# Layer 1's expert stage in 160 tiles of two half tiles with separate experts, instead of 192 tiles of one expert each

## The chip, the cores and the metric

The kernel runs on one core of a Trainium2 chip. The metric is the device time of one execution in microseconds (us). Engines are named as in the profile: PE is TensorE (PEld its weight loads), DVE is VectorE, ACT is ScalarE, POOL is GpSimd, SP is SyncE, which here only issues transfers.

## The reference

Two layers, each a cross attention and a mixture of experts, on 2048 tokens of width 256. The change lies in the experts of layer 1:

```python
def _L1_ffn_ref(x, centroids, expert_biases, Ws_up, Ws_down, W_up, W_down):
    TOP_K = 8                                   # E = 64 experts, D = 256, F = 128, T = 2048
    xf = x.reshape(T, D)
    shared = jax.nn.silu(xf @ Ws_up) @ Ws_down
    aff = xf @ centroids.T
    _, idx = jax.lax.top_k(aff + expert_biases, TOP_K)
    w = jax.nn.sigmoid(jnp.take_along_axis(aff, idx, axis=1))
    w = w / (jnp.sum(w, axis=-1, keepdims=True) + 1e-08)
    cw = jnp.zeros((T, E)).at[jnp.arange(T)[:, None], idx].add(w)
    h = jax.nn.silu(jnp.einsum('td,edf->etf', xf, W_up))
    y = jnp.einsum('etf,efd->etd', h, W_down)
    return (shared + jnp.einsum('etd,te->td', y, cw)).reshape(B, S, D)
```

Each token goes to 8 of 64 experts, which makes 16384 rows of work. A row is a token of width 256, taken up to 128 by its expert, through silu, and back to 256.

## The kernel before, in words

Every engine runs its own instruction list, written out by hand; the lists meet in semaphores alone. During the attention of layer 1, POOL scatters every token's row, together with its 64 gates and 64 places (line 1805), into eight regions of `queue1`, one region per expert. Each region starts with padding rows, so that tiles of full size can be read from it. Then the expert stage runs over NX1 = 192 tiles of 128 rows. A short setup on PE and DVE works out which expert each tile belongs to (`expert_of`) and at which row of `queue1` it starts (`row_of`). The number of tiles is fixed; it doesn't depend on the data.

One tile passes through these steps:

1. SP reads 128 rows of `queue1` into the ring `g1` of 8 buffers (line 428).
2. PE transposes the tile in two halves of the width (`x1_T`, line 959), ACT copies it to `x1T` (line 1217).
3. DVE copies the expert's up weights into `w_now` (`weights_up`, line 1677), and also takes the place and the gate of each row from columns of `g1` that the expert's number picks (`places`, lines 1671 and 1672).
4. PE makes the up product, in which the weights are the stationary operand, so that the result h is already transposed (`up1`, line 974). ACT applies silu and writes `h1T` (line 1223).
5. PE makes the down product (`down1`, line 981), straight from `w_dn1`.
6. ACT (even tiles, line 1231) or DVE (odd tiles, line 1686) multiplies by the gate into the ring `y1` of 8 buffers.
7. POOL scatters the 128 rows to `routed1` by an indirect transfer (line 1848). Padding rows go to dump rows.

The order on PE in round j is up(j), transposes(j+2), down(j-2). The order on DVE is places(j), weights(j+1), and every second round an output. `w_now` holds two tiles' weights, and weights(j+1) waits for up(j-1) alone. Numbers of experts are loaded into registers of PE (line 963) and DVE (line 1689) 24 at a time, and rows' numbers into SP's registers 8 at a time (line 422). After the stage, SP reads the 8 rows of each token back and DVE adds them up (line 1714).

Of the kernel before, what the change touches and what calls it, by code (L numbers as in the profile page):

```python
# [26 lines left out]
P = 128  # L27
# [5 lines left out]
def build(nc, x, ctxT, mask, WqT, bq, Wk, bk, Wv, bv, w_routerT, gate_up, down, w_gateT, w_upT, w_downT,  # L33
# [20 lines left out]
    NX1 = 192  # L54
    assert NX0 >= E0 - 1 + TOK // P and NX1 >= E1 - 1 + TOK * TOP1 // P
# [8 lines left out]
    QROWS = P + TOK  # L64
    FAR = float(1 << 15)
    DUMPS = RING * P
    AHEAD = 16
    HELD = 24
    queue1 = nc.dram_tensor("queue1", [E1 * QROWS, XW], F32).ap()
    routed1 = nc.dram_tensor("routed1", [DUMPS + TOK * TOP1, D], F32).ap()  # L70

    ctx = ExitStack()
    with ctx:
# [8 lines left out]
        for shared, names in (  # L82
# [22 lines left out]
            ("gates1_steps", ("idx_y", "w_col")),  # L105
# [22 lines left out]
        for name, before in (("x1T_ps", "x0T_ps"), ("x1T", "x0T"), ("up1_ps", "eg0_ps"), ("w_now", "sg0x"), ("h1T", "e0T"),  # L128
                             ("dn1_ps", "dn0"), ("y1_1", "y0")):
            LATER[name] = (before, NX0)  # L130
# [32 lines left out]
        iota16 = sb("iota16", [P, NX1], F16)  # L163
        step128 = sb("step128", [P, NT])
        token_id = sb("token_id", [P, NT])
# [19 lines left out]
        ended = sb("ended", [P, NX1], F16)  # L185
# [7 lines left out]
        expert_of = sb("expert_of", [1, NX1], I32)  # L193
# [6 lines left out]
        pos1 = sb("pos1", [1, NX1])  # L200
# [3 lines left out]
        row_of = sb("row_of", [1, NX1], I32)  # L204
        w_col = sb("w_col", [P, AHEAD])
        idx_y = sb("idx_y", [P, AHEAD], I32)
        dump_at = sb("dump_at", [P, RING])
# [86 lines left out]
        g1, y1 = q(RING, XW), q(RING, D)  # L294
        x1T, w_now, h1T = q(2, KC, P), q(2, KC, F1), q(4, P)
        active1, began1, row_at = q(NX1), q(NX1), q(NX1)
# [38 lines left out]
        def _(sp):  # L335
# [22 lines left out]
            queue1_pads = queue1.rearrange("(e r) d -> r e d", e=E1)[0:P]  # L358
            sp.wait_ge(S("pads_made"), 1)
            for t in range(NT):  # L360
                sp.wait_ge(S("xs0"), nth("xs0", t + 1))
                sp.dma_start(scaled0[t * P:(t + 1) * P, :], xs0).then_inc(S("xs0_stored"), 16)
                at = slice(t * E1 // NT, (t + 1) * E1 // NT)
                sp.dma_start(queue1_pads[:, at], pads[:, :].unsqueeze(1).broadcast_to([P, E1 // NT, XW])).then_inc(S("pads_in"), 16)
# [55 lines left out]
            for j in range(NX1):  # L420
                if j % RING == 0:
                    _, at = nc.values_load_multi_w_load_instructions(row_of[0:1, j:j + RING], engines=(sp.engine,), min_val=0, max_val=E1 * QROWS - P,
                                                                     skip_runtime_bounds_check_because="the row names whole tiles of the regions alone")
# [9 lines left out]
            for t in range(NT):  # L433
                if t >= SUMS:
                    sp.wait_ge(S("final"), t - SUMS + 1)
                sp.dma_start(sums1[:, t % SUMS], routed1[DUMPS + t * P * TOP1:DUMPS + (t + 1) * P * TOP1, :].rearrange("(p k) d -> p k d", k=TOP1)).then_inc(S(f"sums_in{t % SUMS}"), 16)
# [93 lines left out]
        def _(pe):  # L530
# [417 lines left out]
            pe.matmul(bank(2)[:, 0:NX1], expert_rep[:, :], active1[0:E1, :], start=True, stop=True).then_inc(S("expert1_ps"), 1)  # L948
            pe.wait_ge(S("shift1"), nth("shift1", 1))
            pe.matmul(bank(0)[0:1, 0:NX1], tiles_of[0:E1, 3:4], active1[0:E1, :], start=True, stop=True).then_inc(S("row1_ps"), 1)  # L950
# [4 lines left out]
            def x1_T(j):  # L955
                k = j % RING
                pe.wait_ge(S(f"x1_in{k}"), nth(f"x1_in{k}", 16 * (j // RING + 1)))
# [4 lines left out]
            def experts(at):  # L962
                _, e = nc.values_load_multi_w_load_instructions(expert_of[0:1, at:at + HELD], engines=(pe.engine,), min_val=0, max_val=E1 - 1,
# [3 lines left out]
            def up1(j):  # L967
# [924 lines left out]
```

## Time and profile before

| | |
|---|---|
| median of 3 runs | 992.81 us (991.91 to 999.23) |
| profiled execution, its own time | 993.83 us |
| its span | 992.0 us |
| PE, DVE, ACT, POOL busy | 830.3, 558.5, 392.7, 408.9 us |
| expert stage of layer 1, first to last scatter of POOL | 692.57 to 936.89 us |
| sums after it | 937 to 992 us |

The chain that ended last spends 49% of the span on PE, 17% on DVE, 9% on POOL and 8% in transfers. Its shares are of the whole span, and the stages have different limits, so that the prediction reads the expert stage by itself.

### The profile page before, as it was taken

The numbers are of one execution on the slowest core, as the hardware profiler recorded it, in microseconds if no ns is written. First come the engines' busy times: TensorE is split into PE (matmuls) and PEld (weight loads), VectorE is DVE, ScalarE is ACT, GpSimd is POOL, SyncE is SP. The second block draws the span as 40 slices with busy tenths as digits, with TensorE's granted clock in tenths as the row PEclk, the third lists the DMA queues.
The fourth block names the chain that finished last, engine by engine and source line by source line (L and its number), as shares of the span: only waits on it lengthen the run. The fifth ranks groups of instructions, "written<-read, shape, count | busy, mean of one in ns | idle before, by whom it ended". The sixth has DMA issues, their size and how long they took to land.

```text
span 992.0 us, 21201 instructions
## 1 busy us (share of the span) xinstructions
PE 830.3 (84%) x6058; PEld 710.6 (72%) x6058; DVE 558.5 (56%) x1924; ACT 392.7 (40%) x1374; POOL 408.9 (41%) x467
## 2 busy tenths in 40 slices
PE   5899999789999998999999999854999998998300
PEld 4788887589999996677777777633988887787300
DVE  3666666512121123587878778641766666665288
ACT  1222222321111114655656665502766665565200
POOL 3100000031111002136676666562777777777600
PEclk9799999789999997899999999965999999999755
DMA  8123223489999972993233322238888887888397
GB/s 265 69 80 112 90 96 111 169 264 328 328 314 318 340 266 61 292 300 107 106 112 110 107 102 107 102 123 286 262 279 260 258 257 246 265 259 261 122 422 317
DMA packets 125103, 205.29 MB, mean 207 GB/s; under 512 B 13392, under 2 KB 100688, under 8 KB 122960
## 3 DMA queue, kind: packets, MB, share of 16 engines
q1 hardware_dynamic: 100880, 143.31, 44.8%
q0 software_dynamic: 19712, 56.65, 15.7%
q10 hardware_dynamic: 4416, 4.20, 1.3%
q8 instruction: 44, 0.72, 0.3%
q14 instruction: 51, 0.42, 0.1%
HBM read 132.93 MB, written 71.17 MB: 206 GB/s over the span
## 4 chain that ended last, share of the span: by engine, by line
PE 49%; DVE 17%; issue 11%; POOL 9%; DMA 8%; ACT 4%; DVEq 1%; SPq 1%; POOLq 0%; ACTq 0%
PE PS L739 10%; POOL routed L1848 7%; PE PS L749 5%; PE PS L974 4%; PE PS L981 4%; DVE R L1714 4%; PE PS L612 4%; DMA routed<-Q,idx_y 3%; PE PS L630 3%; PE PS L861 3%; PE PS L814 3%; ACT R L1152 2%; DMA R<-in_down 2%; PE PS L959 2%; DVE R L1488 2%
## 5 line engine op out<-in xcount | busy, mean ns | idle before, releaser
L1848 POOL DMA_INDIRECT routed<-Q,idx_y x192 | 187.1, 974 | 73.6 <-issue 46.3
L1805 POOL DMA_INDIRECT queue<-Q,slot x128 | 125.6, 981 | 78.2 <-DVE nmax L1482 49.7
L1152 ACT ACTIVATE R<-PS,nmax 128x154 f32<-128x154 f32 x256 | 108.4, 547 | 63.9 <-DVE nmax L1482 63.9
L974 PEld LDWEIGHTS PS<-Q 128*128 128x128 f32 x768 | 115.6, 193 | 25.1 <-ACT Q L1217 8.0
L974 PE MATMUL PS<-Q 128*128 128x128 f32 x768 | 119.5, 279 | 9.8 <-issue 5.5
L981 PE MATMUL PS<-R,Q 128*128 x384 | 118.3, 390 | 8.1 <-ACT Q L1223 5.1
L739 PEld LDWEIGHTS PS<-R 128*128 128x128 f32 x992 | 118.0, 196 | 6.0 <-issue 4.6
L739 PE MATMUL PS<-R 128*128 128x128 f32 x992 | 119.0, 279 | 2.9 <-DMA R<-in_down 1.8
L1677 DVE COPY Q<-R 128x256 f32 x192 | 60.5, 315 | 49.6 <-PE PS L974 29.8
L959 PE MATMUL PS<-ident,Q 128*128 128x128 f32 x384 | 74.5, 277 | 14.6 <-DMA Q<-queue 14.6
L1760 POOL TENSOR_TENSOR rstd<-var_eps,neg_half 128x1 f32<-128x1 f32 x32 | 17.7, 554 | 159.9 <-DVE var_eps L1312 159.7
L1217 ACT ACTIVATE Q<-PS 128x256 f32<-128x256 f32 x192 | 74.0, 385 | 23.9 <-PE PS L959 23.5
L1442 DVE TENSOR_TENSOR R<-R,PS 128x512 f32<-128x512 f32 x31 | 21.4, 689 | 109.4 <-PE PS L739 109.4
L1686 DVE TENSOR_SCALAR Q<-PS,w_col 128x256 f32<-128x256 f32 x96 | 46.3, 482 | 56.1 <-DMA routed<-Q,idx_y 40.2
L1785 POOL DMA_INDIRECT R<-scaled,idx x32 | 30.6, 955 | 106.4 <-PE PS L725 97.9
L1223 ACT ACTIVATE Q<-PS 128x128 f32<-128x128 f32 x192 | 53.0, 276 | 44.6 <-PE PS L974 42.0
L981 PEld LDWEIGHTS PS<-R,Q 128*128 128x128 f32 x384 | 58.1, 191 | 14.7 <-issue 13.9
L612 PE MATMUL PS<-R 128*128 128x128 f32 x512 | 65.4, 282 | 0.0
L1231 ACT ACTIVATE Q<-PS,w_col 128x256 f32<-128x256 f32 x96 | 45.5, 474 | 45.2 <-DMA routed<-Q,idx_y 35.0
L612 PEld LDWEIGHTS PS<-R 128*128 128x128 f32 x512 | 61.5, 196 | 0.1
L959 PEld LDWEIGHTS PS<-ident,Q 128*128 128x128 f32 x384 | 49.0, 144 | 15.5 <-DMA Q<-queue 15.5
L1152 ACT ACTIVATION_READ_ACCUMULATOR R<-PS,nmax 128x1 f32 x256 | 59.3, 232 | 0.0
(269 smaller groups left out, 1568.2 us busy)
## 6 DMA issues: line engine op xcount, KB each, us to landing
Q<-queue SPq DMA_DIRECT2D x192, 192.0 KB
R<-in_gate_up SPq DMA_DIRECT2D x31, 1024.0 KB, 6.6
R<-routed SPq DMA_DIRECT2D x16, 1024.0 KB, 18.2
R<-in_down SPq DMA_DIRECT2D x31, 512.0 KB, 8.8
queue<-pads SPq DMA_DIRECT2D x16, 768.0 KB, 3.6
R<-in_W_up SPq DMA_DIRECT2D x16, 512.0 KB, 7.3
R<-in_W_down SPq DMA_DIRECT2D x8, 1024.0 KB, 11.2
routed<-R SPq DMA_DIRECT2D x31, 128.0 KB
```

The lines of the kernel that those rows point to most:

```text
L612: i = pe.matmul(bank(b)[:, f * P:(f + 1) * P], w[:, c, f * P:(f + 1) * P], xn2T[:, c, :], start=(c == 0), stop=(c == KC - 1))
L739: i = pe.matmul(bank(2 * half + p)[:, f * P:(f + 1) * P], expert_w[k % WB][0][:, c, at:at + P], x0T[:, p, c, :], start=(c == 0), stop=(c = ...
L749: i = pe.matmul(bank(6 + p)[:, 0:D], e0T[:, p, f, :], expert_w[k % WB][1][:, f, :], start=(f == 0), stop=(f == FC0 - 1))
L959: i = pe.transpose(bank(j % 2)[:, c * P:(c + 1) * P], g1[:, k, c * P:(c + 1) * P], ident[:, :])
L974: i = pe.matmul(bank(2 + p)[:, 0:P], w_now[:, p, c, :], x1T[:, p, c, :], start=(c == 0), stop=(c == KC - 1))
L981: pe.matmul(bank(6 + j % 2)[:, 0:D], h1T[:, j % 4, :], w_dn1[:, bass.ts(e, 1), :], start=True, stop=True).then_inc(S("dn1_ps"), 1)
L1152: i = act.activation(prob[:, g % 2].rearrange("p (k h) -> p h k", h=HG)[:, h, :], src, ACT.Exp, bias=nmax2[:, g % 2, h:h + 1], accum_out=d ...
L1217: act.activation(x1T[:, j % 2].rearrange("p c n -> p (c n)"), bank(j % 2)[:, 0:D], ACT.Copy).then_inc(S("x1T"), 1)
L1223: act.activation(h1T[:, j % 4, :], bank(2 + j % 2)[:, 0:P], ACT.Silu).then_inc(S("h1T"), 1)
L1677: dve.tensor_copy(w_now[:, j % 2].rearrange("p c f -> p (c f)"), w_up1[:, bass.ts(e, 1)].rearrange("p o c f -> p (o c f)")).then_inc(S("w_ ...
L1805: pool.indirect_dma_start(out=queue1, out_offset=bass.IndirectOffsetOnAxis(ap=slot1[:, t * TOP1 + k:t * TOP1 + k + 1], axis=0), in_=pay[:, ...
L1848: pool.indirect_dma_start(out=routed1, out_offset=bass.IndirectOffsetOnAxis(ap=idx_y[:, a:a + 1], axis=0), in_=y1[:, k], in_offset=None).t ...
```

## The change: what it does

A tile now is two halves of 64 rows, and each half can belong to any expert. An expert's rows are rounded up to 64 instead of 128, so that 320 half tiles, 160 tiles, hold all of them. What follows from that in the code:

- SP reads each half with a transfer of its own.
- The up product has the tokens as stationary operand: for each half and each half of the width one matmul with 64 stationary columns, four per tile. Its output has tokens in its rows. The first half's weights are read straight from `w_up1`, the second half's from `w_now`.
- ACT's silu writes `h1`; PE transposes it (`h1_T`, line 986), and DVE copies the transpose to `h1T` (line 1701).
- The down product is two matmuls with 64 stationary columns, again with the first half's weights in place and the second half's in `w_now`.
- `w_now` now holds up and down weights of the second half's expert, 512 numbers per partition, for 5 tiles (`weights_b`, line 1695).
- Gate and place lie side by side and are copied by one DVE instruction per half. Padding rows carry a place out of bounds, and POOL's scatter drops them.
- All outputs are ACT's.
- Registers with experts' numbers are loaded 16 at a time, for 8 tiles, by PE and by DVE; SP loads 16 row numbers for 8 tiles.

The order of the instruction lists changes as follows. `ISA` is the sequencer's work on an address that a register holds. The names in the waits are those of reused semaphores: x0T stands for `x1T`, sg0x for `w_now`, e0T for `h1T`, y0 for the outputs, rows_out and rows_in for the loads and scatters of a ring buffer, gates1_steps for places and gates, eg0_ps for the up product, dn0 for the down product, and in the new kernel eu0_ps for `h1`.

PE, one round of the expert stage, before:

```order
L974 MATMUL PS<-Q 128x128 [waits e0T,sg0x,x0T]
L974 MATMUL PS<-Q 128x128
L959 MATMUL PS<-ident,Q 128x128 [waits rows_out1]
L959 MATMUL PS<-ident,Q 128x128
L981 ISA [waits y0,e0T]
L981 MATMUL PS<-R,Q 128x256
```

PE, one round, now:

```order
L976 ISA [waits sg0x,eu0_ps,x0T]
L976 MATMUL PS<-R,Q 64x128
L978 MATMUL PS<-Q 64x128
L976 ISA
L976 MATMUL PS<-R,Q 64x128
L978 MATMUL PS<-Q 64x128
L961 MATMUL PS<-ident,Q 128x128 [waits rows_out7]
L961 MATMUL PS<-ident,Q 128x128
L986 MATMUL PS<-ident,Q 128x128 [waits e0T,eu0_ps]
L992 ISA [waits y0,e0T]
L992 MATMUL PS<-R,Q 64x256
```

Between the transposes of x and the down product there is now the transpose of h of two tiles earlier, and the down product is that of three tiles earlier. Line 993, the second half's down product, follows.

DVE, the same place of the program, before:

```order
L1671 ISA [waits rows_out3]
L1671 TENSOR_SCALAR idx_y<-Q,dump_at 128x1
L1672 ISA
L1672 COPY w_col<-Q 128x1
L1677 ISA [waits eg0_ps]
L1677 COPY Q<-R 128x256
```

DVE, one round with the load of registers in it, now:

```order
L1701 COPY Q<-PS 128x128 [waits dn0,h1T_ps]
L1689 ISA [waits rows_in7,rows_out7]
L1689 COPY gate_place<-Q 64x2
L1689 ISA
L1689 COPY gate_place<-Q 64x2
L1704 TENSOR_LOAD expert_of
L1695 ISA [waits dn0]
L1695 COPY Q<-R 128x512
```

The copy of h (line 1701, of tile j-2) now stands ahead of the gates of tile j and of the weights of tile j+1 (line 1695). It waits for PE's transpose in the same round. The load stands between gates and weights.

The core of the diff:

```diff
-    NX1 = 192
+    H = P // 2
+    NX1 = 160
+    NH1 = 2 * NX1
...
-    HELD = 24
+    HELD = 8
+    LAG = 3
+    WNOW = LAG + 2
...
                 if j >= RING:
                     sp.wait_ge(S("x1T_ps"), nth("x1T_ps", j - RING + 1))
-                    sp.wait_ge(S("w_col"), nth("w_col", j - RING + 1))
-                sp.dma_start(g1[:, k, :], queue1[bass.ds(at[k], P), :]).then_inc(S(f"x1_in{k}"), 16)
+                    sp.wait_ge(S("w_col"), 2 * (j - RING + 1))
+                for a in range(2):
+                    sp.dma_start(g1[a * H:(a + 1) * H, k, :], queue1[bass.ds(at[2 * k + a], H), :]).then_inc(S(f"x1_in{k}"), 16)
...
-            def up1(j):
+            def up1(j, e):
                 p = j % 2
                 pe.wait_ge(S("x1T"), nth("x1T", j + 1))
+                if j >= 2:
+                    pe.wait_ge(S("h1"), nth("h1", j - 1))
                 pe.wait_ge(S("w_now"), nth("w_now", j + 1))
+                for c in range(KC):
+                    pe.matmul(bank(2 + p)[0:H, 0:F1], x1T[:, p, c, 0:H], w_up1[:, bass.ts(e[2 * j], 1), c, :].rearrange("p o f -> p (o f)"),
+                              start=(c == 0), stop=(c == KC - 1), skip_group_check=True)
+                    i = pe.matmul(bank(2 + p)[H:P, 0:F1], x1T[:, p, c, H:P], w_now[:, j % WNOW, 0, c * F1:(c + 1) * F1],
+                                  start=(c == 0), stop=(c == KC - 1), skip_group_check=True)
+                i.then_inc(S("up1_ps"), 1)
+
+            def h1_T(j):
+                pe.wait_ge(S("h1"), nth("h1", j + 1))
                 if j >= 2:
                     pe.wait_ge(S("h1T"), nth("h1T", j - 1))
-                for c in range(KC):
-                    i = pe.matmul(bank(2 + p)[:, 0:P], w_now[:, p, c, :], x1T[:, p, c, :], start=(c == 0), stop=(c == KC - 1))
-                i.then_inc(S("up1_ps"), 1)
+                pe.transpose(bank(4 + j % 2)[:, 0:P], h1[:, j % 4, :], ident[:, :]).then_inc(S("h1T_ps"), 1)
...
-            for j in range(NX1 + 2):
+            for j in range(NX1 + LAG):
+                if j < NX1:
+                    up1(j, e)
                 if j % HELD == HELD - 1 and j + 1 < NX1:
                     e += experts(j + 1)
-                if j < NX1:
-                    up1(j)
                 if j + 2 < NX1:
                     x1_T(j + 2)
-                if j >= 2:
-                    down1(j - 2, e[j - 2])
+                if 2 <= j < NX1 + 2:
+                    h1_T(j - 2)
+                if j >= LAG:
+                    down1(j - LAG, e)
...
-            def weights_up(j, e):
-                if j >= 2:
-                    dve.wait_ge(S("up1_ps"), nth("up1_ps", j - 1))
-                dve.tensor_copy(w_now[:, j % 2].rearrange("p c f -> p (c f)"),
-                                w_up1[:, bass.ts(e, 1)].rearrange("p o c f -> p (o c f)")).then_inc(S("w_now"), 1)
...
+            def weights_b(j, e):
+                if j >= WNOW:
+                    dve.wait_ge(S("dn1_ps"), nth("dn1_ps", j - WNOW + 1))
+                pair = R[:, 0:NUP + E1 * D].rearrange("p (m e f) -> p e m f", m=2, e=E1)
+                dve.tensor_copy(w_now[:, j % WNOW], pair[:, bass.ts(e, 1)].rearrange("p o m f -> p (o m) f")).then_inc(S("w_now"), 1)
+
+            def h1_T(j):
+                dve.wait_ge(S("h1T_ps"), nth("h1T_ps", j + 1))
+                if j >= 4:
+                    dve.wait_ge(S("dn1_ps"), nth("dn1_ps", j - 3))
+                dve.tensor_copy(h1T[:, j % 4, :], bank(4 + j % 2)[:, 0:P]).then_inc(S("h1T"), 1)
...
-            for j in range(NX1 + 3):
+            for i in range(PAY):
+                dve.wait_ge(S(f"queued{i}"), 16 * TOP1 * (NT // PAY))
+            weights_b(0, e[1])
+            for j in range(NX1 + 2):
+                if j >= 2:
+                    h1_T(j - 2)
                 if j < NX1:
-                    places(j, e[j % HELD])
+                    places(j, e[2 * (j % HELD):2 * (j % HELD) + 2])
                     if j % HELD == HELD - 1 and j + 1 < NX1:
                         e = experts(j + 1)
                 if j + 1 < NX1:
-                    weights_up(j + 1, e[(j + 1) % HELD])
-                if j >= 3 and j % 2 == 0:
-                    out_x1(j - 3)
+                    weights_b(j + 1, e[2 * ((j + 1) % HELD) + 1])
...
-                pool.indirect_dma_start(out=routed1, out_offset=bass.IndirectOffsetOnAxis(ap=idx_y[:, a:a + 1], axis=0),
-                                        in_=y1[:, k], in_offset=None).then_inc(S(f"placed{k}"), 16)
+                pool.indirect_dma_start(out=routed1, out_offset=bass.IndirectOffsetOnAxis(ap=gate_place[:, a, 1:2].bitcast(I32), axis=0),
+                                        in_=y1[:, k], in_offset=None, bounds_check=FIRST + TOK * TOP1 - 1, oob_is_err=False).then_inc(S(f"placed{k}"), 16)
```

## Rows read from the trace of the kernel before

**Rows 1.** Busy time by stage; columns as in the first line, x counts instructions.

```profile
core 0: us, PE busy (x) PEld busy (x) DVE busy (x) ACT busy (x) POOL busy (x), PEclk, DMA share, GB/s
693.00:937.00 244.00, 217.19 (x1503) 195.53 (x1502) 148.41 (x722) 147.02 (x469) 185.78 (x192) 0.99 0.78 249
937.00:992.00 55.00, 0.00 (x0) 0.00 (x0) 43.87 (x64) 0.00 (x0) 0.86 (x1) 0.50 0.86 348
```

**Rows 2.** The scatter's line: durations in ns, then idle time before it (us, times).

```profile
L1848 POOL DMA_INDIRECT routed<-Q,idx_y x192: 963/969/1090, 692.6 to 936.9; - x192
  issue: 46.3, 152
```

**Rows 3.** Timeline of POOL: start us, us, engine, line.

```profile
692.57 0.96 POOL L1848 DMA_INDIRECT routed<-Q,idx_y  x1 [15.34 <-ACT Q L1231]
...
935.62 0.96 POOL L1848 DMA_INDIRECT routed<-Q,idx_y  x1 [0.30 <-issue]
936.89 0.97 POOL L1848 DMA_INDIRECT routed<-Q,idx_y  x1 [0.30 <-issue]
```

**Rows 4.** Timeline of PE in the expert stage, one round.

```profile
711.36 0.61 PE L974 MATMUL PS<-Q 128*128 128x128 f32 x4
711.80 0.38 PE L959 MATMUL PS<-ident,Q 128*128 128x128 f32 x2
712.02 0.60 PE L981 MATMUL PS<-R,Q 128*128 x2
712.46 0.61 PE L974 MATMUL PS<-Q 128*128 128x128 f32 x4
```

**Rows 5.** Timeline of the attention of layer 1, around matmuls with 32 stationary columns.

```profile
620.92 0.39 PE L844 MATMUL PS<-R,Q 104*128 104x128 f32 x2
621.24 0.43 PE L846 MATMUL PS<-R,Q 128*32 128x128 f32 x8
621.59 0.66 PE L855 MATMUL PS<-ident,R 128*128 128x128 f32 x4
622.29 0.69 DVE L1501 TENSOR_TENSOR R<-R,PS 128x512 f32<-128x512 f32 x1 [0.54 <-PE PS L855]
```

**Rows 6.** Timeline of DVE in the expert stage, weights, places, weights.

```profile
715.17 0.29 DVE L1677 COPY Q<-R 128x256 f32 x1 [1.84 <-issue]
715.38 0.21 DVE L1671 TENSOR_SCALAR idx_y<-Q,dump_at 128x1 int32 x1
715.51 0.15 DVE L1672 COPY w_col<-Q 128x1 f32 x1
715.65 0.29 DVE L1677 COPY Q<-R 128x256 f32 x1
```

**Rows 7.** The line of the weights' copy: durations in ns, shape.

```profile
L1677 DVE COPY Q<-R x192: 277/294/545, 684.8 to 923.6; 128x256 f32 x192
```

**Rows 8.** Timeline around a load of registers, PE's weight loads and DVE.

```profile
742.69 0.52 PEld L974 LDWEIGHTS PS<-Q 128*128 128x128 f32 x4 [1.71 <-issue]
...
745.08 0.29 DVE L1677 COPY Q<-R 128x256 f32 x1 [1.92 <-issue]
...
745.44 0.52 PEld L974 LDWEIGHTS PS<-Q 128*128 128x128 f32 x4 [1.78 <-issue]
```

**Rows 9.** Timeline, PE's gap at another load of registers.

```profile
714.47 0.52 PEld L974 LDWEIGHTS PS<-Q 128*128 128x128 f32 x4 [1.16 <-ACT Q L1217]
```

**Rows 10.** Register loads by line: durations in ns (min/median/max).

```profile
L963 PEldq TENSOR_LOAD <-expert_of x8: 1771/1830/2156, 682.7 to 894.9; - x8
L1689 DVEq TENSOR_LOAD <-expert_of x8: 1720/1946/2333, 682.8 to 895.1; - x8
L422 SPq TENSOR_LOAD <-row_of x24: 521/564/871, 682.4 to 906.4; - x24
```

**Rows 11.** Busy time in the attention of layer 1 and after it.

```profile
620.00:640.00 20.00, 18.21 (x158) 13.84 (x159) 14.54 (x39) 11.11 (x50) 10.94 (x12) 1.00 0.28 102
740.00:747.00 7.00, 4.25 (x29) 3.38 (x29) 2.65 (x14) 3.15 (x11) 5.48 (x6) 1.00 0.69 221
651.00:660.00 9.00, 5.22 (x14) 3.16 (x12) 2.69 (x9) 0.19 (x1) 3.98 (x5) 0.50 0.20 76
```

**Rows 12.** ACT's and PE's groups in the expert stage, busy us, mean ns.

```profile
L1217 ACT ACTIVATE Q<-PS 128x256 f32<-128x256 f32 x187 | 72.0, 385 | 0.0
...
L1223 ACT ACTIVATE Q<-PS 128x128 f32<-128x128 f32 x189 | 52.1, 276 | 43.9 <-PE PS L974 41.3 <-issue 2.1
...
L1231 ACT ACTIVATE Q<-PS,w_col 128x256 f32<-128x256 f32 x96 | 45.5, 474 | 45.2 <-DMA routed<-Q,idx_y 35.0 <-DVE w_col L1672 4.5 <-DVE idx_y L1671 2.0
```

More of the change, by code:

```diff
@@ L53, in build @@
     COLS0 = 32
[L54 to L55 removed]
+    H = P // 2
+    NX1 = 160
+    NH1 = 2 * NX1
+    assert NX0 >= E0 - 1 + TOK // P and NH1 >= E1 - 1 + TOK * TOP1 // H
     RING = 8
@@ L127, in build @@
             LATER[f"placed{k}"] = (f"rows_in{k}", 16 * GROUPS0)
-        for name, before in (("x1T_ps", "x0T_ps"), ("x1T", "x0T"), ("up1_ps", "eg0_ps"), ("w_now", "sg0x"), ("h1T", "e0T"),
-                             ("dn1_ps", "dn0"), ("y1_1", "y0")):
+        for name, before in (("x1T_ps", "x0T_ps"), ("x1T", "x0T"), ("up1_ps", "eg0_ps"), ("w_now", "sg0x"), ("h1", "eu0_ps"), ("h1T", "e0T"),
+                             ("dn1_ps", "dn0"), ("y1", "y0")):
             LATER[name] = (before, NX0)
@@ L421, in _ @@
                 if j % RING == 0:
-                    _, at = nc.values_load_multi_w_load_instructions(row_of[0:1, j:j + RING], engines=(sp.engine,), min_val=0, max_val=E1 * QROWS - P,
-                                                                     skip_runtime_bounds_check_because="the row names whole tiles of the regions alone")
+                    _, at = nc.values_load_multi_w_load_instructions(row_of[0:1, 2 * j:2 * (j + RING)], engines=(sp.engine,), min_val=0, max_val=E1 * QROWS - H,
+                                                                     skip_runtime_bounds_check_because="the row names whole half tiles of the regions alone")
                 k = j % RING
@@ L979, in down1 @@
                 if j >= 2:
-                    pe.wait_ge(S(f"y1_{j % 2}"), nth(f"y1_{j % 2}", j // 2))
-                pe.matmul(bank(6 + j % 2)[:, 0:D], h1T[:, j % 4, :], w_dn1[:, bass.ts(e, 1), :], start=True, stop=True).then_inc(S("dn1_ps"), 1)
+                    pe.wait_ge(S("y1"), nth("y1", j - 1))
+                pe.matmul(bank(6 + j % 2)[0:H, 0:D], h1T[:, j % 4, 0:H], w_dn1[:, bass.ts(e[2 * j], 1), :], start=True, stop=True, skip_group_check=True)
+                i = pe.matmul(bank(6 + j % 2)[H:P, 0:D], h1T[:, j % 4, H:P], w_now[:, j % WNOW, 1, :], start=True, stop=True, skip_group_check=True)
+                i.then_inc(S("dn1_ps"), 1)
             pe.wait_ge(S("w1_in"), 16 * (E1 // 8) * (KC + 1))
@@ L1239, in _ @@
                     x1_T(j + 2)
-                if j >= 2 and j % 2 == 0:
-                    out_x1(j - 2)
+                if j >= LAG:
+                    out_x1(j - LAG)
             for t in range(NT):
@@ L1628, in _ @@
             step("count1")
-            dve.tensor_scalar(small[0:E1, 0:NT], step128[0:E1, :], count, 0.0, ALU.is_lt, ALU.add, accum_out=ntiles).then_inc(S("ntiles1"), 1)
+            dve.tensor_scalar(small[0:E1, 0:2 * NT], step64[0:E1, :], count, 0.0, ALU.is_lt, ALU.add, accum_out=ntiles).then_inc(S("ntiles1"), 1)
             step("ntiles1")
@@ L1672, in places @@
[L1672 to L1686 removed]
+                for h in range(2):
+                    own = slice(h * H, (h + 1) * H)
+                    both = g1[own, k, D:XW].rearrange("p (two e) -> p e two", two=2)[:, bass.ds(e[h], 1), :]
+                    dve.tensor_copy(gate_place[own, a, :], both.rearrange("p o two -> p (o two)")).then_inc(S("w_col"), 1)
```

94 lines of the change are left out of this document (41 added, 53 removed).

## The prediction

> **What bounds the kernel now.** I read the busy time by stage first, to cut the expert stage out of the span. It is 244 us long, and no engine fills it: PE's records cover 217 us, POOL's 186 [rows 1]. Then the scatter's own line, since POOL waits there least: one scatter takes 0.97 us, and in 152 of 192 cases 0.30 us follow in which POOL waited for nothing the profile shows [rows 2]. The timeline makes that a beat: the last two scatters start at 935.62 and 936.89, 1.27 us apart. From the first, at 692.57, to the last there are 191 intervals in 244.3 us, 1.28 each [rows 3]. So POOL's scatter sets the pace of the whole stage. PE could go a little faster: its round takes 712.46 - 711.36 = 1.10 us [rows 4]. After the stage come 55 us of sums [rows 1], which the change leaves as they are.
>
> If nothing else came to bind, 160 scatters at 1.28 instead of 192 would save 32 x 1.28 = 41 us. The question is whether the new round can be kept within 1.28 us.
>
> **The new round has a closed loop.** The lists show it without any timing. PE's up product of tile j+1 waits for the weights of tile j+1. DVE makes these last in its round j, behind the copy of h of tile j-2, and that copy waits for PE's transpose of h in round j. That transpose stands behind up(j) and the transposes of x. So PE's first part (up, two transposes of x, transpose of h) and DVE's part (copy of h, two gate copies, weights) alternate; they never overlap. The five buffers of `w_now` don't help, as the order on DVE, not the buffers, holds the weights back. Before, weights(j+1) waited only for up(j-1), and no such loop was there. One turn of the loop, step by step:
>
> - Weights written to first weight load on PE: DVE's copy that starts at 745.08 and takes 0.29 ends at 745.37, PE loads at 745.44 [rows 8]. 0.07 us.
> - The up product. Nothing before has 64 stationary columns. The nearest row is the attention's block of eight records with 32 columns: it starts at 621.24, and the next block with the full array starts at 621.59, 0.35 later, where eight records in line at the 0.11 of rows 4 (four of L974 in 711.80 - 711.36 = 0.44) would need 0.88 [rows 4, 5]. So tiles of the array side by side run together, four at a time: two beats of 0.11, and the rest (0.13) is filling and the change between a split and a full array. With 64 columns two run together, so the up product's eight records take four beats: 0.35 + 2 x 0.11 = 0.57 us to the next full block. I add 0.05 for the first weight loads that nothing hides. From below: no such extra and no cost of changing the split, 0.44. From above: halves that don't overlap, 0.88 + 0.13 = 1.01; this is a rival below.
> - Three transposes and the way to DVE. Four transposes started at 621.59, and DVE's reader started at 622.29, 0.70 later [rows 5]. Three make 0.70 - 0.11 = 0.59.
> - DVE from the copy of h to the start of the weights' copy: from 715.17 to 715.65 there is the same pattern, one copy, two small operations with an address in a register, one copy: 0.48 us [rows 6]. The first copy was 256 wide from SBUF, here it is 128 wide from PSUM; the four instructions' issue sets this time (0.13 between the small ones), so I take it as it is.
> - The weights' copy, now 512 wide. 256 take 0.294 [rows 7], 1 takes 0.15 [rows 6]: the slope gives 0.294 + 0.145 = 0.44. Upper end 0.59, twice the row.
>
> Sum: 0.07 + 0.05 + 0.57 + 0.59 + 0.48 + 0.44 = 2.20 us per tile. Bounds of the sum: 2.0 (the low up product, the rest of DVE 0.05 faster) and 2.4 (the copy at 0.59 and a little more latency).
>
> **Beside the loop, at no cost.** Two down matmuls (0.44 plus a change of the array's split) run while DVE has the turn, 0.92 us. ACT has 0.385 + 0.276 + 0.474 = 1.14 us per tile [rows 12], POOL 1.28, SP two transfers instead of one; all are below 2.20, and their feeds are three tiles apart. POOL's waits vanish from the path, and so do the waits for landed scatters. DVE's sums of gates, every tenth tile, fall into its idle half of the loop. If the loop were cut, POOL would be next at 1.28, and PE at about 1.4 (0.44 + 0.22 + 0.11 + 0.44 and two changes of the split). The padding, the wider setup rows (320 instead of 192) and POOL's extra constant cost below 1 us.
>
> **Loads of registers.** Before, 24 numbers took 1.83 us on PE and 1.95 on DVE, 8 numbers 0.56 on SP [rows 10]. Sixteen should take about 1.2. They now come every 8 tiles, 19 times, and both stand in the loop: PE's between up and the transposes, DVE's between gates and weights. They follow each other, as at 742.69 and 745.44, where PE stood 1.71 and then 1.78 us [rows 8]. Of a load of 24, DVE lost 1.92 [rows 8], nearly all, and PE 1.16 where its queue was full [rows 9]. For 16 I take 1.1 on DVE and 0.9 on PE: 2.0 x 19 = 38 us. Bounds 1.3 and 3.0 per pair: 25 to 57 us. In the kernel before, the slack against POOL's beat paid for most of this.
>
> **Sum.** First scatter: three rounds later in the order instead of two and longer rounds, +2.5 us. Then 159 x 2.20 = 350 and 38. Together 390.5 against 244.3: +146. The profiled execution took 993.83 us, so 1140; it lies 1 us above the median of the runs shown, and I keep **1140 us**. With the bounds: 2.5 + 318 + 25 - 244 = +101, 1095 us; 2.5 + 382 + 57 - 244 = +197, 1191 us.
>
> **Rivals.**
> 1. *POOL still sets the beat* (faster). If DVE's list ran ahead of PE's transposes, the round would be 1.28 and the time 993.8 - 41 + 3 = 955 us. For it speaks that each engine alone has less work than 2.2 us; against it, that the order is fixed in both lists. The new kernel ties with the old at a turn of (244.3 - 2.5 - 38) / 159 = 1.28 us with the loads, and of 241.8 / 159 = 1.52 us if the loads cost nothing; below that it is faster. No bound of the loop comes near either. Chance 4%, and 2% that it ends within 1%.
> 2. *The halves don't overlap on PE.* Each up product takes 0.44 longer, +70 us: 1210 us. Against it are rows 5, though these have 32 columns. 6%.
> 3. *TensorE's clock falls to 1.2 GHz.* In a turn of 2.20 us PE streams 0.44 + 0.33 + 0.44 = 1.21 us, 55%, and in a round with loads 1.21 of 4.2. The granted clock was 1.00 in a stretch where PE's records covered 18.2 of 20 us, and also in 7 us with 4.25 us covered, around two stalls; it was 0.50 only where 14 matmul records stand in 9 us [rows 11]. At half the clock, the 0.77 us of streaming in the loop would double: 0.77 x 159 = +122, 1262 us for the whole stage, about 1180 if a third of it is hit. 13%, most of it for a part of the stage.
> The Trainium skill, "TensorE: Matmul & The Clock Gate", Part 4 on the PE-mode transpose, says that transposes don't count as busy the way matmuls do. By that rule the stage would look emptier than it is, since three of its beats are transposes, and rival 3 would be the forecast. The attention of layer 1, with its many transposes, kept 1.00 [rows 11], so I leave it a rival.
> 4. *The loop is shorter than its parts*, because I count latencies twice: a turn of 1.5 to 1.9 us, 1030 to 1090 us. 7%.
>
> **Numbers.** Forecast (1095 to 1191) 68%, rivals as above. The range takes in rival 2 and the milder part of rival 3: **1085 to 1215**. A change of this kernel is told from none at about 1%. Faster by over 1%: 0.04; within 1%: 0.02; slower by over 1%: 0.94.
>
> **What would show it.** Scatters 2.2 us apart with POOL waiting for ACT, ACT for PE; PE's idle time in front of the up product (line 976) put down to DVE's copy of weights (line 1695), and DVE's idle time in front of line 1701 put down to PE's transpose (line 986); both about 0.9 us or more per tile. The eight records of the up product within about 0.6 us would confirm the overlap; 1 us would be rival 2. Gaps of about 1 us on both engines every 8 tiles for the loads. Clock 1.00 in the stage. The prediction is wrong if DVE's weights are done before PE's transpose of the same round.

## The result and the profile after

| | before | changed |
|---|---|---|
| median, both on one chip | 993.76 us (4 runs, 991.91 to 999.23) | 1274.47 us (4 runs, 1265.88 to 1278.06) |
| profiled execution, its own time | 993.83 us | 1277.72 us |
| first to last scatter of the expert stage | 244.3 us | 521.7 us |

The ratio is 1.281, with a 95% interval of 1.278 to 1.285. The change made the kernel slower, as forecast, but by 281 us and not by 146; the time lies 59 us above the range.

The first view is again the busy time by stage, of the changed kernel. It answers to [rows 1].

```profile
core 0: us, PE busy (x) PEld busy (x) DVE busy (x) ACT busy (x) POOL busy (x), PEclk, DMA share, GB/s
0.00:684.00 684.00, 607.32 (x4522) 508.77 (x4522) 363.79 (x1122) 240.77 (x893) 221.84 (x275) 0.94 0.53 171
684.00:1219.00 535.00, 450.46 (x2400) 229.88 (x2400) 172.06 (x706) 182.30 (x481) 154.45 (x158) 0.56 0.30 91
1219.00:1276.00 57.00, 0.00 (x0) 0.00 (x0) 43.87 (x64) 0.23 (x1) 2.28 (x3) 0.51 0.82 331
```

The stage carries the whole difference: the sums after it still take about 55 us. Two things stand in its row. DVE, ACT and POOL are busy for less than 35% each, so none of them has too much work. And the granted clock is 0.56 on average, where it was 0.99. Cut finer, the same view shows that it has two values and nothing between:

```profile
892.90:1118.20 225.30, 196.19 (x979) 99.54 (x981) 69.25 (x285) 73.93 (x196) 63.68 (x65) 0.50 0.29 91
1118.20:1135.20 17.00, 11.81 (x105) 6.24 (x101) 7.50 (x31) 7.51 (x21) 6.84 (x7) 1.00 0.42 128
```

TensorE ran at 1.2 GHz (0.50) for 225 us in a row, then 17 us at 2.4 GHz (1.00). In the 17 us it issued 105 matmuls, 6.2 per us; in the long stretch 4.3 per us, the same work per turn in longer turns.

Next the groups of the expert stage by line: busy us and mean ns of one, then the idle time ahead of them and what ended it.

```profile
L976 PE MATMUL PS<-R,Q 128*64 x640 | 166.9, 411 | 74.1 <-DVE Q L1695 74.1
...
L1866 POOL DMA_INDIRECT routed<-Q,gate_place x160 | 156.7, 980 | 388.2 <-ACT Q L1246 373.6 <-issue 14.6
...
L1701 DVE COPY Q<-PS 128x128 f32<-128x128 f32 x160 | 46.5, 291 | 325.8 <-PE PS L986 325.8
```

PE waits for DVE's weights in front of the up product, DVE waits for PE's transpose of h in front of its copy, and POOL, which set the pace before [rows 2, 3], stands idle for 388 us. The closed loop is there as the prediction drew it. DVE waits 325.8 / 160 = 2.04 us per tile. PE's own wait reads as only 74.1 / 160 = 0.46 us, half of the 0.9 that was forecast for both engines, because at 1.2 GHz its records are longer and cover most of the time in which DVE has the turn: ahead of the up product that starts at 806.39, at full clock, it is 0.72 us, and ahead of the one at 907.46, at half clock, 0.25.

Here is one turn at full clock, from the timeline: the first weight load of the up product, the transposes of x, DVE's copy of h, its two gate copies, the weights' copy, and the next turn's first weight load.

```profile
806.39 0.13 PEld L976 LDWEIGHTS PS<-R,Q 128*64 128x64 f32 x1 [1.17 <-issue]
...
806.99 0.20 PEld L961 LDWEIGHTS PS<-ident,Q 128*128 128x128 f32 x2 [0.17 <-issue]
807.57 0.29 DVE L1701 COPY Q<-PS 128x128 f32<-128x128 f32 x1 [1.42 <-PE PS L986]
807.78 0.36 DVE L1689 COPY gate_place<-Q 64x2 f32 x2
...
808.17 0.43 DVE L1695 COPY Q<-R 128x512 f32 x1
808.84 0.13 PEld L976 LDWEIGHTS PS<-R,Q 128*64 128x64 f32 x1 [1.18 <-issue]
```

And one at half clock:

```profile
904.21 0.18 PEld L976 LDWEIGHTS PS<-R,Q 128*64 128x64 f32 x1 [1.07 <-issue]
...
905.26 0.29 PEld L961 LDWEIGHTS PS<-ident,Q 128*128 128x128 f32 x2 [0.33 <-issue]
906.20 0.29 DVE L1701 COPY Q<-PS 128x128 f32<-128x128 f32 x1 [2.24 <-PE PS L986]
906.41 0.35 DVE L1689 COPY gate_place<-Q 64x2 f32 x2
906.79 0.43 DVE L1695 COPY Q<-R 128x512 f32 x1
907.46 0.18 PEld L976 LDWEIGHTS PS<-R,Q 128*64 128x64 f32 x1 [1.07 <-issue]
```

Read against the prediction's terms, with the median over all turns of that kind without a load of registers (16 at full clock, 117 at half clock) in the last two columns:

| step of the turn | forecast | 806.39 | 904.21 | median, full | median, half |
|---|---|---|---|---|---|
| weights written to first weight load | 0.07 + 0.05 | 0.24 | 0.24 | 0.24 | 0.24 |
| up product, to the transposes | 0.57 | 0.60 | 1.05 | 0.60 | 1.06 |
| transposes, to DVE's copy of h | 0.59 | 0.58 | 0.94 | 0.58 | 0.94 |
| copy of h, to the weights' copy | 0.48 | 0.60 | 0.59 | 0.59 | 0.59 |
| the weights' copy | 0.44 | 0.43 | 0.43 | 0.43 | 0.43 |
| turn | 2.20 | 2.45 | 3.25 | 2.44 | 3.25 |

DVE's steps are the same at both clocks; PE's two steps grow from 1.18 to 2.00. The turns with a load of registers take 4.17 us at full clock (4 of them) and 4.61 at half (15), which is 1.73 and 1.36 us more.

### The profile page after: what moved, and what is told of

Its sections match the earlier page's. It is cut to its first block, busy times and chain, and to the rows that moved or that the text cites. A ratio compares the mean times of both kernels' runs of the same rounds, so it can differ in the third digit from the quotient of the medians.

```text
span 1275.9 us, 23745 instructions
## 1 busy us (share of the span) xinstructions
PE 1057.8 (83%) x6922; PEld 738.6 (58%) x6922; DVE 579.7 (45%) x1892; ACT 423.3 (33%) x1374; POOL 378.6 (30%) x435
## 4 chain that ended last, share of the span: by engine, by line
PE 55%; DVE 20%; issue 13%; ACT 3%; DMA 3%; DVEq 3%; POOL 1%; SPq 1%; POOLq 0%; ACTq 0%
PE PS L976 12%; PE PS L741 8%; PE PS L961 7%; DVE Q L1695 5%; PE PS L751 4%; DVE R L1731 3%; PE PS L614 3%; PE PS L986 3%; PE PS L632 2%; PE PS L816 2%; PE PS L863 2%; DVE gate_place L1689 2%; ACT R L1167 2%; DVE R L1503 1%; PE PS L592 1%
## 5 line engine op out<-in xcount | busy, mean ns | idle before, releaser
L1866 POOL DMA_INDIRECT routed<-Q,gate_place x160 | 156.7, 980 | 388.2 <-ACT Q L1246 373.6
L976 PE MATMUL PS<-R,Q 128*64 x640 | 166.9, 411 | 74.1 <-DVE Q L1695 74.1
L976 PEld LDWEIGHTS PS<-R,Q 128*64 128x64 f32 x640 | 107.2, 205 | 194.7 <-issue 194.5
L1701 DVE COPY Q<-PS 128x128 f32<-128x128 f32 x160 | 46.5, 291 | 325.8 <-PE PS L986 325.8
L978 PE MATMUL PS<-Q 128*64 128x128 f32 x640 | 167.8, 413 | 0.0
L992 PE MATMUL PS<-R,Q 128*64 x320 | 165.6, 618 | 0.8 <-DVE Q L1701 0.8
L993 PE MATMUL PS<-Q 128*64 128x256 f32 x320 | 165.5, 618 | 0.0
L741 PEld LDWEIGHTS PS<-R 128*128 128x128 f32 x992 | 117.9, 195 | 5.0 <-issue 2.3
L1246 ACT ACTIVATE Q<-PS,gate_place 128x256 f32<-128x256 f32 x160 | 75.7, 473 | 128.7 <-PE PS L993 126.5
L978 PEld LDWEIGHTS PS<-Q 128*64 128x64 f32 x640 | 107.3, 206 | 0.0
L1695 DVE COPY Q<-R 128x512 f32 x160 | 68.3, 427 | 37.4 <-PE PS L993 17.1
L992 PEld LDWEIGHTS PS<-R,Q 128*64 128x64 f32 x320 | 43.9, 195 | 49.2 <-issue 48.8
```

The source lines that it names most:

```text
L741: i = pe.matmul(bank(2 * half + p)[:, f * P:(f + 1) * P], expert_w[k % WB][0][:, c, at:at + P], x0T[:, p, c, :], start=(c == 0), stop=(c = ...
L976: pe.matmul(bank(2 + p)[0:H, 0:F1], x1T[:, p, c, 0:H], w_up1[:, bass.ts(e[2 * j], 1), c, :].rearrange("p o f -> p (o f)"), start=(c == 0), ...
L978: i = pe.matmul(bank(2 + p)[H:P, 0:F1], x1T[:, p, c, H:P], w_now[:, j % WNOW, 0, c * F1:(c + 1) * F1], start=(c == 0), stop=(c == KC - 1), ...
L992: pe.matmul(bank(6 + j % 2)[0:H, 0:D], h1T[:, j % 4, 0:H], w_dn1[:, bass.ts(e[2 * j], 1), :], start=True, stop=True, skip_group_check=True)
L993: i = pe.matmul(bank(6 + j % 2)[H:P, 0:D], h1T[:, j % 4, H:P], w_now[:, j % WNOW, 1, :], start=True, stop=True, skip_group_check=True)
L1246: act.activation(y1[:, k], bank(6 + j % 2)[:, 0:D], ACT.Copy, scale=gate_place[:, j % AHEAD, 0:1]).then_inc(S("y1"), 1)
```

## The experiments

Every kernel was timed beside the kernel before on the same chip, and the ratios are to that. Each short diff is against the changed kernel unless it says otherwise.

### The loop cut: weights of the next tile first

```diff
-                    places(j, e[2 * (j % HELD):2 * (j % HELD) + 2])
-                    if j % HELD == HELD - 1 and j + 1 < NX1:
-                        e = experts(j + 1)
-                if j + 1 < NX1:
-                    weights_b(j + 1, e[2 * ((j + 1) % HELD) + 1])
+                    places(j, old[2 * (j % HELD):2 * (j % HELD) + 2])
```

with the load and `weights_b(j + 1, ...)` moved ahead of `h1_T(j - 2)` on DVE. Nothing else is changed.

> The changed kernel with one reordering on DVE: in round j the weights of tile j+1 are copied first, then h of tile j-2, then the gates. Nothing is left out. Theory (a loop of PE and DVE makes PE idle, and the idle PE is granted 1.2 GHz): DVE's trip gets two PE rounds, so the next bound is PE's own work with 64-column halves, about 1.5 us per tile by the full-clock rounds of the changed kernel (0.60 up, 0.48 to the down product, 0.49 down). Clock 1.00 in the stage, 159 x 1.5 + 15 for loads = 254 us between first and last scatter, 1005 us in all (980 to 1030). Rival (matmuls on 64 columns themselves don't hold the clock, however dense): clock about 0.5 in the stage, a PE round near 2.6 us, 1180 us or more.

Measured: 1010.87 us, ratio 1.019 (1.016 to 1.022). The scatters run from 694.10 to 953.24, and the stage's row is

```profile
694.00:953.00 259.00, 240.60 (x2339) 154.97 (x2335) 170.80 (x690) 172.34 (x468) 159.96 (x159) 1.00 0.60 182
```

with the groups

```profile
L1867 POOL DMA_INDIRECT routed<-Q,gate_place x160 | 160.9, 1006 | 119.2 <-issue 64.6 <-ACT Q L1246 54.6
...
L976 PE MATMUL PS<-R,Q 128*64 x640 | 99.3, 278 | 7.4 <-DVE Q L1695 7.1
```

One change of order on DVE was worth 264 of the 281 us. PE's wait for weights falls from 74.1 to 7.4 us, the clock is 1.00 throughout, and PE is now covered for 240.6 of 259 us. On DVE, two turns look so:

```profile
746.44 0.43 DVE L1695 COPY Q<-R 128x512 f32 x1
...
747.24 0.29 DVE L1701 COPY Q<-PS 128x128 f32<-128x128 f32 x1 [0.37 <-PE PS L986]
747.44 0.35 DVE L1689 COPY gate_place<-Q 64x2 f32 x2
...
747.94 0.43 DVE L1695 COPY Q<-R 128x512 f32 x1
```

The weights' copies start 1.50 us apart, PE's own round now. But this run doesn't say how much was the loop at full clock and how much was the clock, since both went together. The next one holds the loop and changes only the clock.

### The loop kept, TensorE given work in its idle time

```diff
+                if j < NX1:
+                    if j:
+                        pe.wait_ge(S("h1"), nth("h1", j))
+                    for _ in range(2):
+                        pe.matmul(bank(2 + (j + 1) % 2)[:, 2 * P:3 * P], ident[:, :], ident[:, :], start=True, stop=True, skip_group_check=True)
```

at the end of PE's round: two 128x128 products that nobody reads, in the time in which DVE has the turn.

> The changed kernel, order untouched, plus two 128x128 matmuls on the full array per round behind the down product, whose result nobody reads. Theory (low use of PE, made by the loop, costs the clock): the filler runs while DVE has its turn, the clock stays at 1.00, and the round is the 2.44 us that the changed kernel shows at full clock: 159 x 2.44 + 19 x 1.7 = 420 us between the scatters, 1170 us in all (1150 to 1195), 100 us faster than without the filler although PE does more. Rival (the clock has another cause): no gain, 1275 to 1300 us.

Measured: 1183.57 us, ratio 1.192 (1.188 to 1.197). With more work for PE the kernel is 91 us faster than the change. Its stage:

```profile
695.00:1127.00 432.00, 381.64 (x2970) 232.56 (x2966) 169.09 (x691) 177.54 (x469) 156.78 (x159) 0.97 0.36 109
```

The granted clock is 0.97 instead of 0.56, and 128 turns at full clock have a median of 2.45 us, those of the change at full clock. So the 281 us divide into 190 for the loop at (nearly) full clock and 91 for the clock.

### The same with transposes as the filler

```diff
+                    for _ in range(4):
+                        pe.transpose(bank(2 + (j + 1) % 2)[:, 2 * P:3 * P], ident[:, :], ident[:, :])
```

in the place of the two products.

> The changed kernel with filler again, as in the filler kernel and at its place, but four transposes of 128x128 instead of two matmuls; both stream for 0.44 us at full clock. If the clock follows PE's use whatever is streamed: clock about 1.00 in the stage and 1184 us like the matmul filler. If transposes don't count as use, as the Trainium skill says on the PE-mode transpose: the clock stays as low as without filler, PE's added work gets longer, and the time is 1275 us or more.

Measured: 1182.17 us, ratio 1.191 (1.187 to 1.195), and

```profile
695.00:1127.00 432.00, 372.81 (x2968) 216.66 (x2966) 169.65 (x691) 177.52 (x469) 157.08 (x159) 0.97 0.36 109
```

Transposes held the clock as the products did, 0.97. The Trainium skill ("TensorE: Matmul & The Clock Gate", Part 4, on the PE-mode transpose) says of the bf16 transposes measured there that they don't count as busy in the same way. By that rule this kernel, with fp32 transposes, would have kept the change's clock of 0.56; it did not, and the measurement decides. Rival 3 came true, but not for the reason for which the prediction quoted that page. What the change lacked was work on PE between its turns, and either kind would do.

### Half a cut: places and gates behind the weights

```diff
-                if j < NX1:
-                    places(j, e[2 * (j % HELD):2 * (j % HELD) + 2])
...
+                if j < NX1:
+                    places(j, old[2 * (j % HELD):2 * (j % HELD) + 2])
```

The gates move behind `weights_b(j + 1, ...)`; the copy of h stays ahead of it, so the loop stays closed.

> The changed kernel with the two gate copies moved behind the weights on DVE; copy of h still ahead of the weights, so the loop stays, 0.35 us shorter (0.59 to about 0.24 between the copy of h and the weights). Loop theory: 159 x 0.35 = 55 us less at the clock as it is, 1220 us; if the denser PE is granted the full clock for longer, down to 1110. Rival (DVE's order doesn't matter, since PE's matmuls set the round): no change, 1275 us.

Measured: 1162.71 us, ratio 1.171 (1.167 to 1.176), between the two expected values. The turn without a load is 2.21 us at full clock (median of 94) and 2.99 at half; the step from the copy of h to the weights is 0.32 instead of 0.59. The stage's clock:

```profile
697.00:1107.00 410.00, 304.03 (x2346) 161.72 (x2342) 176.74 (x691) 177.53 (x469) 156.25 (x160) 0.90 0.38 115
```

The gates cost 0.27 us of the turn, of which some is lost again to weights' copies that now take longer (next section). 159 x 0.27 = 43 us would be the most at an unchanged clock, but the kernel gained 112 against the change, with full clock in most of the stage (0.90 on average instead of 0.56). A few tenths in a loop moved the clock, and the clock moved more time than they did.

### The loop put into the kernel before

```diff
+                if 1 <= j < NX1 - 1:
+                    dve.wait_ge(S("x1T_ps"), nth("x1T_ps", j + 2))
```

in `weights_up` of the kernel before (diff against that): DVE's weights of tile j+1 now also wait for PE's transposes of tile j+2, which stand behind up(j) in PE's list. It does no work of the change.

> The kernel before with one wait more on DVE: the weights of tile j+1 wait for PE's transposes of tile j+2 in round j, so that the same kind of loop exists without half tiles. Loop theory: a turn of 0.07 + 0.93 on PE + 0.1 + 0.29 on DVE = 1.4 us against POOL's 1.28, 192 x 1.4 + 20 for loads, which are in the loop now, = 290 us for 244: 1040 us (1020 to 1060), clock 1.00, as PE still streams 1.1 of 1.4 us. Rival (POOL or PE hides it): 994 us.

Measured: 1071.73 us, ratio 1.080 (1.075 to 1.084). The wait alone costs 79 us, and the expectation was too low by 12 us at its upper end. In the timeline of DVE the turns differ:

```profile
731.19 0.29 DVE L1679 COPY Q<-R 128x256 f32 x1 [1.66 <-PE PS L959]
...
732.70 0.29 DVE L1679 COPY Q<-R 128x256 f32 x1 [1.01 <-PE PS L959]
732.91 0.48 DVE L1688 TENSOR_SCALAR Q<-PS,w_col 128x256 f32<-128x256 f32 x1
733.30 0.20 DVE L1671 TENSOR_SCALAR idx_y<-Q,dump_at 128x1 int32 x1
733.42 0.14 DVE L1672 COPY w_col<-Q 128x1 f32 x1
734.21 0.51 DVE L1679 COPY Q<-R 128x256 f32 x1 [0.64 <-PE PS L959]
```

The weights come 1.51 us apart here, and PE's up products start at 731.59, 733.09 and 734.82, 1.50 and then 1.73 apart: a turn with an output (L1688) in it is followed by a weights' copy of 0.51 instead of 0.29 and a later product. The expectation had 1.4 us for every turn; without an output it is 1.51, and the turns with one were not priced at all. The longer copy falls into a scatter of POOL, here the one that starts 0.55 us before it:

```profile
733.66 0.97 POOL L1850 DMA_INDIRECT routed<-Q,idx_y  x1 [1.80 <-DVE Q L1688]
```

In this kernel 80 of the 192 weights' copies start 0.5 to 0.6 us after a scatter did; they take 0.51 us (median), and none of the other 112 takes more than 0.30. In the kernel with the gates moved, 70 of 160 copies start 0.5 to 0.8 us after a scatter did, and every one of them ends 1.23 us after the scatter's start, whenever it began, so that they take 0.43 to 0.70 us. A copy that starts in the second half of a scatter is thus held until 0.1 to 0.25 us after the scatter's recorded end. In the change only one weights' copy starts within a scatter, and all take 0.43. The clock stayed at 0.99 in this kernel, so it is a measure of a loop alone.

### What bounds it once the loop is cut: the loads

The cut kernel's turn is 1.50 us, and 2.2 in every eighth. Here PE loads the first halves' experts only, 8 numbers from a row of their own, on top of the cut:

```diff
-                _, e = nc.values_load_multi_w_load_instructions(expert_of[0:1, 2 * at:2 * (at + HELD)], engines=(pe.engine,), min_val=0, max_val=E1 - 1,
+                _, e = nc.values_load_multi_w_load_instructions(expert_a[0:1, at:at + HELD], engines=(pe.engine,), min_val=0, max_val=E1 - 1,
```

> The kernel with the weights first on DVE, and PE loads only what it needs, the expert of each first half: 8 numbers instead of 16 per 8 tiles, from a row of its own. Nothing is left out. If loads of registers stand in PE's path, where that kernel's round with a load took 2.34 us against 1.50: a load of 0.56 instead of 1.11 us gives back 19 x 0.5 = 10 us: 1001 us (997 to 1006). Rival (the round with a load is long because of DVE's own load of 16): no change, 1011 us.

Measured: 1013.01 us, ratio 1.020 (1.017 to 1.023): no change against the cut kernel's 1.019. PE's load did become 0.61 us, and the turn with the load is still 2.17 us. DVE's load, still of 16 numbers, accounts for most of it: PE waits 9.5 us for DVE's weights in the stage (23 waits), and 19 turns that are 0.67 us too long make 13 us. The two loads:

```profile
L966 PEldq TENSOR_LOAD <-expert_a x20: 590/612/1018, 681.5 to 937.6; - x20
...
L1706 DVEq TENSOR_LOAD <-expert_of x20: 1095/1241/1457, 681.5 to 937.3; - x20
```

### Two tiles per round

```diff
-    LAG = 3
-    WNOW = LAG + 2
+    LAG = 4
+    WNOW = 7
...
+            for j in range(0, NX1 + LAG, 2):
+                for i in (j, j + 1):
+                    if i < NX1:
+                        up1(i, e)
```

and so on for every step of PE, ACT and DVE, with the weights first and PE's short load: the array would change its split half as often.

> The same kernel with two tiles per round on PE, ACT and DVE: two up products, then four transposes of x, two of h, then two down products; w_now has 7 buffers, the lag is 4 tiles. Nothing is left out. If PE's own work, with the changes between the split and the full array, is what bounds the weights-first kernel (1.50 us per tile): one pair of changes per two tiles instead of per tile saves 0.1 us, 159 x 1.40 + 19 x 0.5 + 4 = 236 us between the scatters, 985 us (970 to 998), under both kernels. Rival (the two waits inside a round on DVE or ACT bind instead): 1000 us or more.

Measured: 1033.31 us, ratio 1.041 (1.039 to 1.044), slower than the cut kernel by 22 us where 26 less were expected. On DVE, with two weights' copies in a row:

```profile
802.29 0.49 DVE L1712 COPY Q<-PS 128x128 f32<-128x128 f32 x2 [0.42 <-PE PS L989]
802.69 0.88 DVE L1700 COPY gate_place<-Q 64x2 f32 x4
803.61 0.76 DVE L1706 COPY Q<-R 128x512 f32 x2
805.67 0.49 DVE L1712 COPY Q<-PS 128x128 f32<-128x128 f32 x2 [1.30 <-issue]
```

The pair takes 3.38 us, 1.69 per tile, where the cut kernel takes 1.50. PE's up product waits 41.9 us in the stage: 22.5 for DVE's weights and 19.1 for ACT. So the coarser hand-over between the engines cost more than fewer changes of the split can have bought; what those bought by themselves no run shows.

### Weights two tiles ahead

On top of the kernel with PE's short load:

```diff
-    WNOW = LAG + 2
+    WNOW = LAG + 3
...
+            weights_b(1, e[3])
...
+                if j + 2 < NX1:
+                    weights_b(j + 2, e[2 * (j + 2) + 1])
```

> The weights-first kernel with PE's short load, and DVE's weights copied two tiles ahead instead of one (6 buffers of w_now); DVE's load of 16 numbers so comes one round earlier too. Nothing is left out. With one tile ahead, PE's rounds are 1.50 us, but 2.2 us every eighth, where DVE loads registers for 1.2 us. If it is DVE's load that PE meets there: the second tile of lead covers it, 19 x 0.6 = 11 us less, 1002 us, and 995 if the rounds of 1.65 us in between shorten too. Rival (these rounds are long for another reason, PE's own queue or the outputs): no change, 1013 us.

Measured: 1079.39 us beside 1072.33 for the kernel before, ratio 1.006 (1.004 to 1.009). The chip was another one, on which the kernel before itself took 79 us longer than on the others. So this ratio can't be set against the 1.020 of above, and both kernels went once more, together:

> The kernel of x8 (weights copied two tiles ahead, TensorE loads 8 numbers), now on the same chip as x5's kernel. If the second weights' place ahead of the loop is what one tile more of distance buys, the loads' long turns (2.17 us against 1.5) shrink to 1.5 and seven or eight us of the loop go: ratio to the kernel before 1.00 to 1.01 where x5 had 1.0199, and about 0.013 below x5's kernel of this call. If another wait has taken the turn over (ScalarE's output copies, or the scatters), both have the same ratio within 0.004.

> The kernel of x5 again, as the measure of x9 on this chip: ratio to the kernel before 1.017 to 1.023 as it was, if the chip is like the first; on a chip whose transfers are slower, nearer to 1.00, since the stages ahead then weigh more and the scatters hide the loop.

Measured, on yet another chip, where the kernel before takes 1084.41 us: two ahead 1085.54 us, ratio 1.001 (0.998 to 1.003); one ahead 1090.41 us, ratio 1.005 (1.002 to 1.007). The ratios are 0.0039 apart where the first theory expected 0.013, and their intervals touch. On this chip that is the second theory's answer, though only just within its 0.004. But here the whole stage is longer, for a reason that stays open (below), and that can hide what the second tile of distance buys. The kernel with weights two tiles ahead was never timed on a chip like the first, so whether it gives back the 11 us there stays open. On such a slow chip the cut kernel with PE's short load is within 1% of the kernel before. No version of the change beat it anywhere.

### The two kernels once more

> The kernel before, unchanged, for its profile on whatever chip this call gets: on two chips it took 1072 and 1084 us instead of 993. If the chip is such a one, its expert stage should be 50 to 60 us longer at the same busy time of each engine, as it is in x9 and x10; if it is one like the first, the span is 992 us again.

> The change unchanged. On a chip like the first, 1274 us and ratio 1.28. On one where the kernel before takes 1075 us: if what such a chip adds falls into the changed loop's idle times, about 1300 us and a ratio of 1.21; if it adds to the loop, 1350 us and 1.26.

Measured, on another chip, where the kernel before is as fast as at first: it took 992.35 us (one run), the change 1291.12 us (4 runs) beside 992.32 (7 runs), ratio 1.300 (1.294 to 1.306). What the slow chips add could not be seen. But the change took 17 us more than the first time, and the row of its stage says why:

```profile
684.00:1235.00 551.00, 480.58 (x2400) 243.03 (x2400) 170.73 (x705) 182.43 (x481) 154.30 (x158) 0.50 0.29 89
```

In this execution no turn of the loop was at full clock after the first scatter; the first profile had 0.56 for the stage. Why one execution got stretches at full clock and the other none stays open. Its scatters are 539.8 us apart from first to last, and turns of 3.25 us (140) and 4.60 us (19 with loads) add up to 542. This is rival 3 for the whole stage. Against the filler's 1183.57 us the clock costs 107.6 us when it never rises.

## Why the prediction was wrong, and where it was right

**The step that failed** is the clock. The prediction took 1.00 for the stage, gave the fall to 1.2 GHz 13%, "most of it for a part of the stage", and argued that the attention of layer 1 kept 1.00 [rows 11]. That row showed a stretch in which PE's records cover 18.2 of 20 us; it could not speak for a loop in which, by the prediction's own sum, PE streams 1.21 of each 2.20 us, for 350 us and more. The other row at 1.00 covers 7 us around two stalls, against a loop of hundreds. The half-clock row (14 matmuls in 9 us) was a real warning, and it was put aside. Measured were 0.56 in one profile and 0.50 in the other, with plain turns of 3.25 us instead of 2.44. The filler kernels showed the cost: 91 us in one set of runs, 107.6 in the other where the clock never rose. The price of the rival itself, 0.77 us per turn and 122 for the stage, was near: measured are 3.25 - 2.44 = 0.81 per plain turn, and less in turns with loads (4.61 - 4.17 = 0.44).

**The mechanism was right.** A closed loop of PE and DVE, not POOL, sets the pace; the waits are ahead of lines 976 and 1701 and of POOL's scatter (line 1866), as forecast. Cutting it on DVE alone brought the stage from 521.7 to 259.1 us. Putting a similar one into the kernel before cost 79 us with no other change.

**The turn was 0.24 us too short.** With the clock held the prediction would still have missed: 1183.57 us against 1140, though inside the range. Of the 44 us, 159 x 0.25 = 40 are the turn; the loads give back 5, and the rest, some 9, is left for the few turns that fell to half clock there (0.97). Two terms carry the 0.25. From the weights to PE's first weight load it takes 0.24 instead of 0.12: the row that I took it from [rows 8] has a matmul whose operand has a fixed address, and in the new kernel work on an address in a register follows the wait. That this work is the 0.12 is read from the order of the lists; no run changes it alone. And from the copy of h to the weights it takes 0.59 instead of 0.48: two gate copies stand where the old row had two other operations [rows 6], and I took the old distance as it was. The up product (0.60 for 0.57), the transposes (0.58 for 0.59) and the weights' copy (0.43 for 0.44) were right, so rival 2 was wrong: the halves do run side by side, eight records with 64 columns in 0.60 us.

**The loads** were 1.73 us at full clock for 2.0, 33 us for 38; at half clock 1.36. The difference lies on PE: in a turn with a load, it takes 1.29 us from the up product's first weight load to the transposes at either clock, which is 0.69 more than without a load at full clock (0.60) and 0.23 more at half (1.06), where the up product runs on under more of the load. The two loads themselves took 1.10 on PE and 1.21 on DVE where 1.2 was the estimate; PE's cost to the turn was 0.69 and not 0.9.

**The first scatter** came at 695.1 with the filler, 2.5 us later than before, as forecast, and at 699.2 in the change, at half clock.

The sum for the filler kernel then closes: 2.5 for the first scatter, scatters over 432.2 us instead of 244.3, so +190 against 190.98 measured (1183.57 - 992.59). The change's profiled execution closes too: 6.7 for the first scatter and 277.4 for the stage make 284.1 of 283.9 us (1277.72 - 993.83).

**Rival 1** (POOL's beat) and **rival 4** (a shorter loop) were wrong. The prediction's remark on what comes next when the loop is cut, PE at about 1.4 us, was near: 1.50.

## What to carry to other kernels

When two engines take turns, first look whether one of them issues the step that the other waits for behind a step that waits for the other: here one change of order in DVE's list gave back 264 of 281 us. Then price the turn at both levels of TensorE's clock, because a loop that leaves PE idle in each turn may not get the full one: the stage's clock was 0.56 and 0.50 in the change, 0.90 with 0.27 us less in each turn, and 0.97 with work in PE's idle time. And a latency read from a matmul with a fixed address (0.07 us) need not hold for one whose address is in a register (0.24).

## What the runs showed of the hardware that was not expected

- TensorE's granted clock stayed at 0.50 over 539 us of a loop in which it issued 4.4 matmuls per us and waited in every turn. With four records of unread work per turn, some 0.44 us at the 0.11 of a record, it was 0.97, whether of products or of transposes, and the kernel was 91 us faster.
- The same kernel had 0.56 and 0.50 as its stage's clock in two profiled executions, and its medians in the two sets of runs were 1274 and 1291 us.
- Loads of registers from SBUF: 16 numbers take 1.10 us on PE and 1.2 on DVE, 8 numbers 0.61 on PE. With 24 at 1.83 and 1.95 [rows 10], that is about 0.07 us a number.
- The weights' copies of DVE (fp32, from SBUF to SBUF) that start in the second half of a scatter of POOL's are held until shortly after its end: all 70 of them end 1.23 us after the start of a scatter of 0.98 in the kernel with the gates moved.
- Chips differ more than the change of some kernels: the kernel before took 992 to 994 us in four sets of runs, on at least three chips, 1072 us on another and 1084 on a further one. One kernel, the cut one with PE's short load, has a profile on a chip of each kind, and its stage reads (columns as in the first view), where the kernel before takes 993 and where it takes 1084 us:

```profile
694.00:957.00 263.00, 242.29 (x2342) 155.37 (x2342) 172.50 (x690) 172.69 (x469) 160.30 (x160) 1.00 0.59 180
...
715.00:1041.00 326.00, 263.46 (x2340) 158.63 (x2339) 168.25 (x690) 155.35 (x468) 161.29 (x160) 0.96 0.48 145
```

Its scatters take 261.4 us from first to last on the one and 325.1 on the other, so that 64 of the 84 us between the two profiled executions fall into this stage. Only PE is busy for longer, by 21 us; the rest is idle time on every engine. What causes it stays open: no profile of the kernel before was had on such a chip.
